# Attention head fills: key slots of the stacks crossed between the row halves, 12 transfers a head in place of 32, and a wait for each kind

## The reference

```python
def _L0_attn_ref(hidden_states, Wq, Wk, Wv, Wo, rel_bias):      # B, S, D = 2, 2048, 512; H, DK = 16, 64
    def proj(W):
        return (hidden_states @ W.T).reshape(B, S, H, DK).transpose(0, 2, 1, 3)
    q, k, v = (proj(Wq), proj(Wk), proj(Wv))
    scores = jnp.einsum('bhqd,bhkd->bhqk', q, k)
    scores = scores + rel_bias[_relative_position_buckets(S)].transpose(2, 0, 1)[None]
    attn = jax.nn.softmax(scores, axis=-1)
    ctx = jnp.einsum('bhqk,bhkd->bhqd', attn, v)
    return ctx.transpose(0, 2, 1, 3).reshape(B, S, H * DK) @ Wo.T
x = x + _L0_attn_ref(_layernorm(x, axis=-1), ...)
x = x + _L0_xattn_ref(_layernorm(x, axis=-1), ctx_1024, ctx_1024, mask, ...)
x = x + _L0_ffn_ref(_layernorm(x, axis=-1), ...)
```

## Time and profile before

| | |
|---|---|
| three runs | 4177.5, 4181.5, 4183.55 us, median 4181.5 |
| the profiled execution | 4169.57 us, of which the span is 4167.8 us |
| mean granted TensorE clock | 0.958 |
| busy in the span | PE 90%, PEld 53%, DVE 59%, ACT 48%, POOL 64% |
| fill transfers | 512 of c_k, 256 of c_q, 256 of c_d: 32 a head, 128 KB each |
| one head | about 92 us (the waits that come back once a head start 91 to 92 us apart) |

### The profile page before, as it was taken

One profiled execution on the slowest core, in us unless ns is written; L12 is line 12 of the kernel. 1 busy time (PEld: TensorE's weight loads), 2 busy tenths in 40 slices (PEclk: granted clock), 3 DMA queues, 4 the chain that ended last, 5 costly groups with the idle time before them and its releaser, 6 DMA issues. The chain is left out here.

```text
span 4167.8 us, 64834 instructions
## 1 busy us (share of the span) xinstructions
PE 3766.1 (90%) x21277; PEld 2217.3 (53%) x21277; DVE 2448.8 (59%) x3356; ACT 1989.7 (48%) x3452; POOL 2678.3 (64%) x1402
## 2 busy tenths in 40 slices
PE   8989998989999898899998889998997999997899
PEld 6844444444444444444444444444444888885477
DVE  3466656655656565556656555656652777775642
ACT  3335555555555554555555555555553455553322
POOL 1138888878888887788888878888896344441010
PEclk9989999999999999999999999999999999999999
DMA  8632223332222253322223332222232233335720
GB/s 227 164 90 61 61 62 70 85 81 62 65 61 61 65 157 87 70 64 63 61 62 71 82 84 61 66 61 61 61 106 82 79 106 99 103 99 173 250 79 21
DMA packets 407284, 367.05 MB, mean 88 GB/s; under 512 B 199579, under 2 KB 271771, under 8 KB 405784
## 3 DMA queue, kind: packets, MB, share of 16 engines
q1 hardware_dynamic: 337976, 336.54, 31.4%
q10 hardware_dynamic: 67168, 20.98, 2.2%
q0 software_dynamic: 1920, 6.29, 0.5%
HBM read 142.64 MB, written 89.70 MB: 56 GB/s over the span
## 5 line engine op out<-in xcount | busy, mean ns | idle before, releaser
L344 POOL TENSOR_TENSOR acc<-acc,probs 128x1024 f32<-128x1024 f32 x894 | 2125.4, 2377 | 517.9 <-ACT probs L802 324.6
L932 DVE TENSOR_REDUCE maxes<-ps 128x2 f32<-128x1024 f32 x1024 | 1251.9, 1223 | 784.2 <-PE ps L601 765.4
L805 ACT ACTIVATE probs<-ps,far_bias 128x1024 f32<-128x1024 f32 (+7 forms) x1280 | 997.6, 819 | 1142.2 <-DVE near_s L949 617.6
L632 PE MATMUL ps<-probs,v_head 128*64 128x512 f32 x4096 | 1045.0, 633 | 6.9 <-ACT ctx_out L788 4.9
L620 PE MATMUL ps<-stacks 64*128 64x512 f32 x6144 | 814.3, 393 | 1.8 <-ACT probs L802 1.8
L601 PE MATMUL ps<-stacks 64*128 64x512 f32 x2048 | 520.2, 506 | 303.2 <-DVE maxes L932 279.0
L601 PEld LDWEIGHTS ps<-stacks 64*128 64x128 f32 x2048 | 196.8, 189 | 888.1 <-DVE maxes L932 672.3
L620 PEld LDWEIGHTS ps<-stacks 64*128 64x128 f32 x6144 | 587.4, 188 | 127.6 <-ACT probs L802 7.5
L632 PEld LDWEIGHTS ps<-probs,v_head 128*64 128x64 f32 x4096 | 257.3, 141 | 475.2 <-issue 470.8
L949 DVE TENSOR_TENSOR near_s<-ps,near_bias 128x384 f32<-128x384 f32 (+2 forms) x576 | 262.2, 489 | 37.7 <-PE ps L620 37.3
L802 ACT ACTIVATE probs<-near_s 128x384 f32<-128x384 f32 (+2 forms) x576 | 273.6, 475 | 0.0
(11 more groups left out here) (278 smaller groups left out, 4502.7 us busy)
## 6 DMA issues: line engine op xcount, KB each, us to landing
stacks<-c_k SPq DMA_DIRECT2D x512, 128.0 KB, 2.4
stacks<-c_q SPq DMA_DIRECT2D x256, 128.0 KB, 2.4
stacks<-c_d SPq DMA_DIRECT2D x256, 128.0 KB, 2.4
scr_v<-probs ACTq DMA_DIRECT2D x32, 512.0 KB, 4.1
v_head<-scr_v SPq DMA_DIRECT2D x32, 512.0 KB, 3.6
scr_ctx<-ctx_out SPq DMA_DIRECT2D x128, 128.0 KB, 2.3
both_ctx<-scr_ctx SPq DMA_DIRECT2D x32, 512.0 KB, 3.9
sums<-scr_inv SPq DMA_DIRECT2D x126, 128.0 KB, 2.9
```

The lines of the kernel that those rows point to most:

```text
L344: pool.tensor_tensor(acc[:, qb, :], acc[:, qb, :], pr, ALU.add).then_inc(s["summed"], 1)
L632: mm = pe.matmul(ps[64 * half:64 * half + 64, PV, :], v_head[:, side, kt, :], probs[:, st % PT_RING, half * 512:(half + 1) * 512], start=k ...
L805: ins = act.activation(probs[:, st % PT_RING, a:z], sc[:, a:z], ACT.Exp, bias=bias)
L932: dve.tensor_reduce(maxes[:, qt:qt + HALF_GROUPS // 2 + 1:HALF_GROUPS // 2, first_chunk + pair], ps[:, bank:bank + 2, :], AX.X, ALU.max).t ...
```

## The change

The tiles c_q, c_k and c_d are kept. The slots KL and KH are replaced with KA and KB: KA is a straight copy of all 128 rows of c_k, KB the same with its halves exchanged. High keys then stand in KA for the lower rows and in KB for the upper ones, low keys the other way round, which the matmuls pick by half. Queries go in 4 transfers, keys in 3 for the first three blocks and 3 for the last, c_d in 2: 12 a head, with the same bytes. There are three semaphores: fill_q (awaited by `take_out` of the next projected head), fill_k (by its `keys_out`) and fill_d (by its `step_hi`, and by `scores` at the beginning of a head). `largest` now waits for fill_q and all of fill_k. `take_out`, `queries_low` and `keys_out` move one group earlier, into the group of the projection (2, 6, 10, 14); `step` and `step_hi` move to groups 3, 7, 11, 15; `step_lo` stays one group later (4, 8, 12, and 0 of the next head), now ahead of `largest` of pair 1.

```diff
--- before.py
+++ after.py
@@ -66,8 +66,9 @@
 
 TERMS = [(k, i, j) for k in range(KT) for i, j in ((0, 0), (0, 1), (1, 0))]
 PROJ_GROUPS = {4 * tb + 2: (tb, 0, len(TERMS)) for tb in range(BLOCKS)}
-EVAC_GROUPS = {4 * tb + 3: tb for tb in range(BLOCKS)}
-SPLIT_GROUPS = {4 * (tb + 1) % GROUPS: tb for tb in range(BLOCKS)}
+EVAC_GROUPS = {4 * tb + 2: tb for tb in range(BLOCKS)}
+STEP_GROUPS = {4 * tb + 3: tb for tb in range(BLOCKS)}
+LOW_GROUPS = {4 * (tb + 1) % GROUPS: tb for tb in range(BLOCKS)}
 FIRST_MAX, LAST_MAX = 3, 2
 SUM_GROUPS = {13: 0, 5: 1}
 RECIP_GROUPS = {14: 0, 6: 1}
@@ -104,7 +105,7 @@
 
 QUARTERS = 4
 QUARTER, QP = QW // QUARTERS, P // QUARTERS
-FILLS_MAX, FILLS_SCORE, FILLS_GUARD = 16 * 3 * BLOCKS, 16 * 5 * BLOCKS, 32
+FILLS_Q, FILLS_K, FILLS_D, FILLS_GUARD = 16 * 4, 16 * 6, 16 * 2, 32
 CHUNKS = S // 512
 
 
@@ -175,7 +176,8 @@
 
 
         xn_hi, xn_lo, stacks = [homes[n] for n in ("xn_hi", "xn_lo", "stacks")]
-        KD, KL, KH, QS = range(4)
+        KD, KA, KB, QS = range(4)
+        KH, KL = (KA, KB), (KB, KA)
         QL = S // 2
         guard_keys = sb("guard_keys", [P, QBLK, P], F32R)
         guard_q = sb("guard_q", [P, 512], F32R)
@@ -225,6 +227,14 @@
             homes[n] for n in "wo wo_hi wo_lo wq2 wk2 wv2 enc bv bk k2 v2 ctx x bq".split()]
 
 
+        def queries(side, half, at):
+
+            return stacks[lane(half), side, QS, at:at + QL].rearrange("p (b n) -> p b n", n=512)
+
+        def own_queries(rows, half):
+
+            return rows.rearrange("p (b a n) -> p a b n", a=2, n=512)[:, half, :, :]
+
         def proj_bank(m, tb):
 
             return (PB, SC, SC + 1, MX + 1)[tb] if isinstance(m, int) and m == 0 else PB
@@ -240,7 +250,7 @@
 
         names = """const_ready consts_in bias_max bias_table bias_mm bias_stored wv_hi wv_lo stat
             moment rstd1 rstd2 xn turned xhi xlo vps vout w_in w_hi w_split
-            proj q_hi k_own k_hi q_lo step step_hi step_lo fill_max fill_score
+            proj q_hi k_own k_hi q_lo step step_hi step_lo fill_q fill_k fill_d
             maxed max_done neg_ready neg_stored neg_in
             scored biased exped summed pved summ sum_out spread recip recip_stored recip_in
             ctx_raw ctx near_tab held ctx_stored zeros lead kv_in wo_in wq2_in rows_in
@@ -399,22 +409,20 @@
                 past(sp, s["scored"], (m - 1) * STEPS)
                 if isinstance(m, int) and m == 1:
                     sp.wait_ge(s["vps"], N_HALVES)
-                for tb in range(BLOCKS):
-                    cols = slice(tb * 512, (tb + 1) * 512)
-                    q_high = slice(tb // 2 * 512, (tb // 2 + 1) * 512)
-                    sp.wait_ge(s["k_hi"], 4 * m + tb + 1)
-                    sp.wait_ge(s["step_lo"], 4 * m + tb + 1)
+                sp.wait_ge(s["q_lo"], 4 * m + BLOCKS)
+                for own in range(2):
                     for half in range(2):
-                        sp.dma_start(stacks[lane(half), side, KH, cols].bitcast(F32), c_k[0:64, cols]).then_inc(s["fill_max"], 16)
-                    sp.dma_start(stacks[lane(tb % 2), side, QS, q_high].bitcast(F32), c_q[0:64, cols]).then_inc(s["fill_max"], 16)
-                for tb in range(BLOCKS):
-                    cols = slice(tb * 512, (tb + 1) * 512)
-                    own = slice(LOOKBACK + tb * 512, LOOKBACK + (tb + 1) * 512)
-                    q_low = slice(QL + tb // 2 * 512, QL + (tb // 2 + 1) * 512)
+                        part = half ^ own
+                        sp.dma_start(queries(side, half, QL * part).bitcast(F32), own_queries(c_q[lane(part), :], half)).then_inc(s["fill_q"], 16)
+                for first, end in ((0, BLOCKS - 1), (BLOCKS - 1, BLOCKS)):
+                    cols = slice(first * 512, end * 512)
+                    sp.wait_ge(s["k_hi"], 4 * m + end)
+                    sp.wait_ge(s["step_lo"], 4 * m + end)
+                    sp.dma_start(stacks[:, side, KA, cols].bitcast(F32), c_k[:, cols]).then_inc(s["fill_k"], 16)
                     for half in range(2):
-                        sp.dma_start(stacks[lane(half), side, KD, cols].bitcast(F32), c_d[0:64, own]).then_inc(s["fill_score"], 16)
-                        sp.dma_start(stacks[lane(half), side, KL, cols].bitcast(F32), c_k[64:128, cols]).then_inc(s["fill_score"], 16)
-                    sp.dma_start(stacks[lane(tb % 2), side, QS, q_low].bitcast(F32), c_q[64:128, cols]).then_inc(s["fill_score"], 16)
+                        sp.dma_start(stacks[lane(half), side, KB, cols].bitcast(F32), c_k[lane(1 - half), cols]).then_inc(s["fill_k"], 16)
+                for half in range(2):
+                    sp.dma_start(stacks[lane(half), side, KD, :].bitcast(F32), c_d[0:64, LOOKBACK:]).then_inc(s["fill_d"], 16)
 
             def divisors(n, qb):
 
@@ -590,7 +598,8 @@
                 m, mside = (n + 1, 1 - side) if late else (n, side)
                 qt, first_chunk = max_tiles(turn)
                 if late and g == FIRST_MAX and pair == 0:
-                    pe.wait_ge(s["fill_max"], FILLS_MAX * (m + 1))
+                    pe.wait_ge(s["fill_q"], FILLS_Q * (m + 1))
+                    pe.wait_ge(s["fill_k"], FILLS_K * (m + 1))
                 if isinstance(n, int) and n < 0:
                     past(pe, s["max_done"], 2 * turn + pair - 1)
                 else:
@@ -598,7 +607,7 @@
                 q = slice((qt // 8 * 4 + qt % 8) * P, (qt // 8 * 4 + qt % 8 + 1) * P)
                 keys = slice((first_chunk + pair) * 512, (first_chunk + pair + 1) * 512)
                 for half in range(2):
-                    mm = pe.matmul(ps[:, max_bank(n, pair) + half, :], stacks[lane(half), mside, QS, q], stacks[lane(half), mside, KH, keys],
+                    mm = pe.matmul(ps[:, max_bank(n, pair) + half, :], stacks[lane(half), mside, QS, q], stacks[lane(half), mside, KH[half], keys],
                                    start=True, stop=True)
                 mm.then_inc(s["maxed"], 1)
 
@@ -615,9 +624,9 @@
                         pe.wait_ge(s["neg_in"], FILLS_GUARD * (2 * n + qb + 1))
                     for half in range(2):
                         pe.matmul(ps[:, bank + half, :], guard_keys[lane(half), qb, :], guard_q[lane(half), :], start=True, stop=True)
-                for of_keys, of_queries in ((KD, q_high), (KD, q_low), (KL, q_high)):
+                for of_keys, of_queries in (((KD, KD), q_high), ((KD, KD), q_low), (KL, q_high)):
                     for half in range(2):
-                        mm = pe.matmul(ps[:, bank + half, :], stacks[lane(half), side, of_keys, keys], stacks[lane(half), side, QS, of_queries],
+                        mm = pe.matmul(ps[:, bank + half, :], stacks[lane(half), side, of_keys[half], keys], stacks[lane(half), side, QS, of_queries],
                                        start=False, stop=True, skip_group_check=True)
                 mm.then_inc(s["scored"], 1)
 
@@ -689,7 +698,7 @@
                         largest(n, side, g, 0)
                     if own:
                         if g == 0:
-                            pe.wait_ge(s["fill_score"], FILLS_SCORE * (n + 1))
+                            pe.wait_ge(s["fill_d"], FILLS_D * (n + 1))
                         scores(n, side, 2 * g)
                         scores(n, side, 2 * g + 1)
                     if has_max(n, g):
@@ -760,19 +769,22 @@
                 cols = slice(tb * 512, (tb + 1) * 512)
                 act.wait_ge(s["proj"], 4 * m + tb + 1)
                 if tb == 0:
-                    past(act, s["fill_max"], FILLS_MAX * m)
-                    past(act, s["fill_score"], FILLS_SCORE * m)
+                    past(act, s["fill_q"], FILLS_Q * m)
                 act.copy(c_q[0:64, cols].bitcast(F32R), ps[0:64, proj_bank(m, tb), :]).then_inc(s["q_hi"], 1)
 
             def keys_out(m, tb):
 
                 bank = proj_bank(m, tb)
+                if tb == 0:
+                    past(act, s["fill_k"], FILLS_K * m)
                 act.copy(c_d[64:128, LOOKBACK + tb * 512:LOOKBACK + (tb + 1) * 512], ps[64:128, bank, :]).then_inc(s["k_own"], 1)
                 act.copy(c_k[0:64, tb * 512:(tb + 1) * 512].bitcast(F32R), ps[64:128, bank, :]).then_inc(s["k_hi"], 1)
 
             def step_hi(m, tb):
 
                 act.wait_ge(s["step"], 4 * m + tb + 1)
+                if tb == 0:
+                    past(act, s["fill_d"], FILLS_D * m)
                 act.copy(c_d[0:64, LOOKBACK + tb * 512:LOOKBACK + (tb + 1) * 512].bitcast(F32R), ps[0:64, proj_bank(m, tb), :]).then_inc(s["step_hi"], 1)
 
             def sums_out(n, qb):
@@ -842,15 +854,10 @@
                     if own:
                         exp(n, k, side, 2 * g)
                         exp(n, k, side, 2 * g + 1)
+                    if prep and g in STEP_GROUPS:
+                        step_hi(n + 2, STEP_GROUPS[g])
                     if prep and g in EVAC_GROUPS:
                         take_out(n + 2, EVAC_GROUPS[g])
-                    if g in SPLIT_GROUPS:
-                        tb = SPLIT_GROUPS[g]
```

(23 more changed lines are left out.)

## The result

The changed kernel takes 3973.21 us (median of 4 runs, 3972.2 to 3976.46), the kernel before 4182.52 us (4 runs): a ratio of 0.9502, 95% interval 0.9486 to 0.9519. Forecast were 3950 us and 3865 to 4065. The profiled execution took 3972.34 us, its span 3970.6 us.

A forecast was written before the change was run, and what follows sets the result against it. TensorE, 90% busy, was held by a fill limited by SP's issue. A head gains 6.83 + 2.3 + 0.8 - 2.1 = 7.8 us, 226 in 29 heads, plus 5 in head 30: 231, so 4181.5 becomes 3950 us, range 3865 to 4065.

The forecast's parts named there:

- The likeliest case: Keys land near 14 us after the fill's start and the clock holds: 3950 us, own range 3915 to 3990, chance 0.5.
- The condition that the clock is held: TensorE's clock would not fall in the 2.1 us wait before group 3, since a matmul after 2.31 us idle took 0.50.
- old stall in group 4: PE's idle time before pair 1 of group 4, 6.83 us a head, 198.0 us in 29 heads, would go.
- PE's busy time, by the clock: The lower clock after the stall, lasting into the next group, cost 2.3 us a head, which would be won.
- small waits for the reduction: PE's waits of at most 1 us for VectorE, 1.8 us a head: 0.8 would be won back, bounds 0 and 1.8.
- new wait for the keys: PE would wait 2.1 us a head before `largest` in group 3, for all of fill_k; bounds 0 and 3.8.
- The moved wait: `take_out` would wait only for the 4 query transfers, already landed in group 2, so 6.83 us a head goes.
- The time the data takes: Straight copies at 363 GB/s, 64-row ones at 224: keys land 14.1 us after the fill's start, bounds 9.7 and 15.8.
- The issues that go: 12 transfers at 0.64 us take SP 7.7 us instead of 20.5; nothing on the path is charged for SP's time.
- Head 30: Its stall of 4.71 us, VectorE waiting for a small transfer issued behind the fill, would go: 5 us with the clock.
- the longer wait with a fallen clock: Rival: straight copies no faster than 64-row ones, PE waits 3.8 us in group 3, clock falls: 4065 us, chance 0.24.
- no wait at all: Rival: all copies at 396 GB/s, keys land at 9.7 us, no PE wait in group 3: 3890 us, chance 0.18.

## Why the prediction was right, and where 23 us went

The likeliest case came true in its main steps: the wait that held `take_out` was the stall, its place is taken by a shorter wait in group 3, and the copies' rates set that. The condition that the clock is held did not come true. The measured median is 23 us above the forecast. The terms come from the profiled executions, and there the miss is larger: 4169.57 to 3972.34 us is 197, where 231 were forecast, 34 less. The profiled execution of the kernel before stands 13 us below its median and that of the changed kernel 1, so some 11 us of the nearness are luck. To see which terms carry the 34, take the stretch from the first fill inside the heads to the last, 29 heads (356.6 to 3023.3 us before, 352.8 to 2819.9 after), and add up PE's idle times in it by what ended them. The stretch shrank by 199.6 us, where the terms of the forecast come to 227; head 30 (5 us, below) and the rest of the span (2) make up what is left of the 34.

| term, 29 heads | forecast | measured |
|---|---|---|
| old stall in group 4 (and the 3.99 in the reload head) | -198 | -202.0 |
| PE's busy time, by the clock | -67 | -44 |
| small waits for the reduction (54.6 to 43.0) | -23 | -11.6 |
| new wait for the keys (11.8 of it in the reload head) | +61 | +47.9 |
| waits marked "issue" at a head's start (19.1 to 28.6) | 0 | +9.5 |

The clock's line is the difference of PE's busy time in the two stretches, before and after, since the instructions are the same:

```profile
357.00:3023.30 2666.30, 2389.52 (x13224) 1191.03 (x13224) 1598.19 (x1914) 1376.05 (x2289) 2171.65 (x958) 0.95 0.31 72
```
```profile
352.80:2819.90 2467.10, 2345.17 (x13226) 1185.67 (x13224) 1615.17 (x1915) 1391.60 (x2290) 2174.48 (x958) 0.99 0.32 78
```

2389.5 - 2345.2 = 44.3 us. The lines add up to 200.

- **The moved wait**: right. With one wait for all kinds the kernel is 215 us slower again, the whole gain.
- **The time the data takes**: right in the sum (14.1 against 14.2 us), and near in its two rates: 363 taken for straight copies and 356 measured over 2.5 us, 224 for 64 rows and 233 measured. At first the queries go slower (146 GB/s from 1804 to 1807 us, while they start), for which the 1.8 us at the end of the sum seem to have made room. That 64 rows and 128 rows differ was the choice that mattered: as two halves the keys landed at 15.7, where 15.8 was the bound worked out for it.
- **The issues that go**: I charged nothing for SP and was right for a wrong reason. SP took 12.7 us for the 12 transfers, not 7.7; once transfers queue up, a single issue takes up to 2.22 us (at 1810.97). It didn't matter, as far as the keys show, since it only kept pace with the data.
- **The new wait**: 1.9 to 2.5 us, as forecast, but in 14 of the 29 heads only. In the reload head it is 11.78, with the slow clock after it (0.79 for the matmul), where I had given nothing for the reload; before the change a wait of 3.99 for the queries stood there. A wait of over 4 us with a slow clock is what I had named as a sign of being wrong; it holds in this head and in head 30.

```profile
1478.80 0.79 PE L610 MATMUL ps<-stacks 64*128 64x512 f32 x2 [11.78 <-DMA stacks<-c_k]
```

In the other 14, PE stands idle 1.7 to 2.3 us at the head's start ("issue"); after that the keys are in time in eight and 0.6 to 1.1 us late in six. So the sum came out 13 us smaller, and the growth of the "issue" waits, which I had left out, took 9.5 back. They grew by 0.6 us each, from 1.5 to 2.0. They came with the moved groups: with the groups put back they are 21.9 us in 14 (1.6 each), with the order alone put back 28.8. By which path, no run settles.
- **The clock**: "no fall after 2.1 us" was wrong in more heads than not. Two heads whose waits for the keys were 2.45 and 2.50 us long, in windows that begin 0.7 us after the first matmul:

```profile
1989.00:1992.00 3.00, 3.00 (x16) 1.78 (x14) 2.32 (x4) 1.91 (x4) 0.14 (x1) 0.50 0.98 199
2329.00:2332.00 3.00, 3.00 (x22) 1.28 (x18) 2.94 (x5) 1.91 (x4) 0.17 (x1) 1.00 0.95 199
```
```profile
1988.31 0.50 PE L610 MATMUL ps<-stacks 64*128 64x512 f32 x2 [2.45 <-DMA stacks<-c_k]
...
1993.78 0.50 PE L610 MATMUL ps<-stacks 64*128 64x512 f32 x2
...
2328.29 0.50 PE L610 MATMUL ps<-stacks 64*128 64x512 f32 x2 [2.50 <-DMA stacks<-c_k]
...
2332.89 0.50 PE L610 MATMUL ps<-stacks 64*128 64x512 f32 x2 [0.42 <-DVE maxes L939]
```

The first matmul takes 0.50 us in both, and then the clock of the first falls to 1.2 GHz. Group 3 lasts 5.5 us there and 4.2 here without its 0.42 of idle time: a fall costs 1.3. It happened in 9 of the 14 heads with a wait of 1.9 to 2.5 us. The row that I had rested on (2.31 us, then a matmul of 0.50, in the earlier trace rows) could not show it, because one matmul right after the wait doesn't tell. The clock fell in the same way after 7 of the 14 "issue" waits at a head's start, and before the change after 1 of 13. Two such heads, with waits of 2.19 and 2.35 us that ended at 520.27 and 689.48:

```profile
521.00:524.00 3.00, 3.00 (x18) 2.15 (x14) 1.53 (x3) 1.21 (x2) 3.00 (x3) 0.54 0.40 87
690.00:693.00 3.00, 3.00 (x22) 1.79 (x22) 2.64 (x4) 1.27 (x3) 3.00 (x3) 1.00 0.39 84
```

Group 0 lasts 6.1 us in the first and 4.6 in the second without its idle time, so a fall costs 1.5 there. The six heads with late keys (0.6 to 1.1 us) are all among the seven in which the clock held: in the others the fall had cost more than that already. The 44 us in the table are thus, as an estimate, about 65 won and some 21 lost again (9 x 1.3, and 1.5 for each of the six falls after "issue" waits that are new), so the old fall cost about 2.2 a head, near the 2.3 that I took. What failed is the step that no new fall comes.
- **The small waits**: this step failed in its reason. I wrote that `step_lo` alone in its group would give 0.8 us back. The change also put it ahead of the reduction of pair 1, and PE's next pair 0 waits for that one:

```profile
1866.74 0.69 DVE L975 TENSOR_TENSOR c_k<-ps,c_d 64x512 fp32r<-64x512 f32 x1
1867.46 1.23 DVE L939 TENSOR_REDUCE maxes<-ps 128x2 f32<-128x1024 f32 x1
```
```profile
1868.74 0.49 PE L610 MATMUL ps<-stacks 64*128 64x512 f32 x2 [0.53 <-DVE maxes L939]
```

With the order of before, PE's wait for the reduction is 29.2 us over the whole span, where the forecast left 52.1 - 23 = 29: the new order took away what I had counted on. The size of the term was wrong all the same: with the old order and the old groups these waits come to 118, so the moved groups are worth 1.9 us a head and not 0.8. That the time of that run, 3947, is 3 us from the forecast is luck in part, since its wait for keys (70.8) is longer than forecast.

- **Head 30** was a miss: its 4.71 us for a small transfer went, but 5.13 us for the keys came. It has no projection in group 2, and it reaches group 3 some 9.4 us after its fill's start (2819.86), 2.4 us sooner than the head at 1818.24.

Of the rivals, no wait at all would have needed all copies at 396 GB/s; the 64-row ones reach 233 to 249. Of the longer wait with a fallen clock, only the fallen clock came true, in about half of the heads. The Trainium skill ("DMA: Bandwidth & Descriptors", section "Where 436 GB/s comes from") lets 435 GB/s bind every copy on the chip; here only the straight ones come near it, with 424 in their best microsecond.

## What to carry to other kernels

When one buffer is read by several transfers and rewritten by several writers, give each writer the wait for the transfers that read its part, and order the transfers by who is needed first: here taking that away lost the whole gain, and the fewer, longer transfers were worth 110 us beside it. Then ask of each wait which bytes it is for; TensorE waited for low keys that it never reads in that stage, and sending those last was worth another 33 us, 79 with the queue behind it put right. An instruction moved ahead of a reduction costs time as soon as another engine waits for that reduction, even if it waits for nothing itself (26 us here). And after a wait, read the clock over the next few microseconds and not from the first matmul.

## What the runs showed of the hardware that I had not expected

- Copies on the chip from 128 rows to the same 128 rows ran at 424 GB/s in their best microsecond and at 356 over 2.5 us, copies from 64 to 64 rows at 233 to 249 over 2.5 to 7 us (1812.5 to 1815 of the changed kernel, 1658 to 1665 with the straight copies as halves), all at a full share of the DMA engines. The 224 read from a queue limited by issue was an underestimate by at most a tenth.
- An issue on SP costs 0.6 us while the transfers keep up, and up to 2.22 us in the fill shown when they are behind. v_head (512 KB), behind the fill, took 2.12 us to issue at 1816.96 and a median of 8.5 us to land, where it was 3.6 before the change.
- After idle times of TensorE of 1.9 to 2.5 us that a transfer ended, the granted clock fell to 1.2 GHz in 9 heads, in 7 of them only some time after the first matmul, and stayed at 2.4 GHz in 5, the longest of all (2.50) among them. After those of 1.7 to 2.4 us marked "issue" it fell in 7 heads and stayed in 7.
